# Keys and values from rounded parts of the context, scan units in other slots, a pair's end two slots later, sums over two units

## Time and profile before

| | |
|---|---|
| time, median of 3 runs | 2230.54 us (2229.82 to 2233.25) |
| profiled execution | 2231.84 us, its span 2230.1 us |
| busy in the span | PE 2087.4 us (94%), DVE 1631.8 (73%), ACT 1519.4 (68%), POOL 597.7 (27%) |
| maxima of strips (L989) | 256, 1827 ns each |
| keys (L597), values (L607), turnings (L632) on PE | 399.0, 406.1, 464.4 us busy |

### The profile page before, as it was taken

The page is one execution under the profiler, slowest core; times in us unless marked ns, Lnnn a source line. Parts: engine busy times, 40 slices in busy tenths (PEclk is TensorE's granted clock), DMA queues, the critical chain, the costliest instruction groups (busy, mean ns, idle before and its releaser), DMA issues. The chain is left out here.

```text
span 2230.1 us, 54255 instructions
## 1 busy us (share of the span) xinstructions
PE 2087.4 (94%) x20746; PEld 1431.6 (64%) x20746; DVE 1631.8 (73%) x3522; ACT 1519.4 (68%) x3140; POOL 597.7 (27%) x604
## 2 busy tenths in 40 slices
PE   7999999999999999999999999999998559989965
PEld 4666666666666666666666666666665448868854
DVE  4447777878787878687878787777778747767746
ACT  2667776767686868676767777777768237757753
POOL 0001030303030312122121213030303127767770
PEclk9999999999999999999999999999999569999988
DMA  6475762213232222222222222221201147666748
GB/s 214 172 264 213 263 215 102 98 48 101 63 92 74 73 74 73 75 76 74 72 79 67 83 75 87 77 93 53 99 16 60 63 132 222 211 223 210 220 131 339
DMA packets 114271, 277.26 MB, mean 124 GB/s; under 512 B 19851, under 2 KB 70711, under 8 KB 107872
## 3 DMA queue, kind: packets, MB, share of 16 engines
q1 hardware_dynamic: 95584, 239.10, 32.7%
q0 software_dynamic: 18432, 34.69, 4.4%
HBM read 165.40 MB, written 108.27 MB: 123 GB/s over the span
## 5 line engine op out<-in xcount | busy, mean ns | idle before, releaser
L989 DVE TENSOR_REDUCE sb_negmax<-S 128x1 f32<-128x1604 f32 x256 | 467.7, 1827 | 145.6 <-PE S L622 139.7
L808 ACT ACTIVATE sb_probsT<-W 128x384 f32<-128x384 f32 (+1 forms) x1024 | 476.1, 516 | 90.7 <-PE W L632 86.5
L816 ACT ACTIVATE sb_probs<-S,sb_negmax 128x1604 f32<-128x1604 f32 x256 | 409.3, 1599 | 113.1 <-DVE sb_negmax L989 113.0
L632 PEld LDWEIGHTS W<-sb_ident,sb_probs 128*128 128x128 f32 (+1 forms) x3328 | 365.4, 139 | 185.8 <-ACT sb_K L800 133.3
L632 PE MATMUL W<-sb_ident,sb_probs 128*128 128x128 f32 (+1 forms) x3328 | 464.4, 278 | 6.5 <-ACT sb_probsT L808 2.5
L607 PE MATMUL W<-sb_wkv_in,sb_ctx 128*128 128x256 f32 (+1 forms) x1664 | 406.1, 386 | 14.3 <-ACT sb_probsT L808 12.4
L597 PE MATMUL W<-sb_ctx,sb_wkv_in 128*32 128x401 f32 x4096 | 399.0, 503 | 1.5 <-DMA sb_ctx<-ctxT 1.5
L800 ACT ACTIVATE sb_K<-W,sb_pair_cols 128x401 f32<-128x401 f32 x256 | 152.7, 596 | 279.9 <-PE W L597 279.8
L607 PEld LDWEIGHTS W<-sb_wkv_in,sb_ctx 128*128 128x128 f32 (+1 forms) x1664 | 293.4, 187 | 74.2 <-ACT sb_probsT L808 38.2
L1369 POOL DMA_INDIRECT y_scratch<-sb_ys,sb_places x256 | 254.0, 992 | 109.1 <-issue 74.4
L622 PE MATMUL S<-sb_K,sb_Q 32*128 32x400 f32 (+1 forms) x2048 | 244.3, 546 | 7.3 <-ACT sb_probs L816 6.1
(11 more groups left out here) (197 smaller groups left out, 2813.4 us busy)
## 6 DMA issues: line engine op xcount, KB each, us to landing
sb_ctx<-ctxT SPq DMA_DIRECT2D x32, 1604.0 KB, 7.6
xe_scratch<-sb_none SPq DMA_DIRECT2D x32, 1088.0 KB, 12.2
sb_xg<-xe_scratch SPq DMA_DIRECT2D x64, 544.0 KB, 4.1
sb_BC<-bc_scratch SPq DMA_DIRECT2D x32, 1024.0 KB, 6.2
sb_Q<-sb_q_own SPq DMA_DIRECT2D x128, 128.0 KB, 4.1
y_scratch<-sb_none SPq DMA_DIRECT2D x16, 1024.0 KB, 12.0
sb_rows<-y_scratch SPq DMA_DIRECT2D x16, 1024.0 KB, 8.1
sb_wgu<-wgu SPq DMA_DIRECT2D x64, 192.0 KB
```

What stands on the lines that cost most here:

```text
L632: ins = pe.transpose(W[0:keys_in(t), at * P:(at + 1) * P], probs[n % 2][:, t * P:t * P + keys_in(t)], ident[:])
L808: act.activation(probsT[k][n % (k + 1)][:, 0:wide], ring[bank_of("T", G, k)][:, 0:wide], ACT.Copy)\
L816: act.activation(probs[n % 2][:].rearrange("p (c k) -> p c k", c=QUADS), scores_of, ACT.Exp, bias=negmax[:, slot:slot + 1], accum_out=den[ ...
L989: dve.tensor_reduce(negmax[:, slot:slot + 1], scores_of, AX.XY, ALU.max, negate=True).then_inc(max_done, 1)
```

## The change

*Rounded parts.* The weights of keys and values and each batch's context are split into a rounded part (float32r, written by a ScalarE copy) and a remainder (VectorE subtraction, also float32r). Keys and values are made of three products, hi x hi, lo x hi and hi x lo, by two feature halves: six matmuls in place of two. The context comes in quarters of 402 columns (128 x 804 elements with both feature halves) into one buffer; `part_ctx` (ScalarE) and `part_low` (VectorE) take a quarter in the slots of `PART_AT`, SyncE loads the next batch's quarter in the slots of `LOAD_AT`.

*Keys of four strips at once.* A job K is now one quarter of the context for all 128 features of a group, so four jobs give four strips. They go to K_f, and SyncE deals each strip's 32 rows with four transfers into one of four K tiles. Keys are made six strips ahead (`LEAD`) in place of four.

*Slots.* The scan units move to `UNIT_AT`; the end of a pair (m 13 to 15) comes two slots later (`LATE`), yT in slot 3, ln3T and logits in slot 4, the choice in slot 5; values move from slots 1 to 7 and 9 to 15 to slots 2 to 8, 10 to 15 and 0; XQ and Q move to slot 9, Q behind the keys.

*Sums.* Two units' products are added first, then summed over states once; three instructions per unit become four per two units.

The diff, its core:

```diff
-NO_VALUES = (0, 8)
+NO_VALUES = ()
-CK = (M + QUADS - 1) // QUADS
+CK = 2 * ((M + 2 * QUADS - 1) // (2 * QUADS))
+LEAD = 6
+OF = 4
+PART_AT = {1: (1, 0), 2: (1, 1), 3: (1, 2), 4: (1, 3), 7: (2, 0), 8: (2, 1), 10: (2, 2), 11: (2, 3)}
+LOAD_AT = {2: (2, 0), 3: (2, 1), 4: (2, 2), 5: (2, 3), 8: (3, 0), 9: (3, 1), 11: (3, 2), 12: (3, 3)}
+LATE = 2
+END = SLOTS * (PAIRS + 1) + LAG + LATE
 MIX = {(4, 0): ["O3"], (5, 0): ["oqT"], (5, 1): ["proj"], (6, 0): ["ln2T"], (6, 1): ["xp"], (7, 0): ["dt"],
-       (8, 0): ["XQ"], (8, 1): ["Q"], (10, 0): ["O0"], (14, 0): ["O1"], (1, 0): ["yT"],
-       (2, 0): ["O2", "ln3T"], (2, 1): ["logits"], (3, 2): ["pos"]}
+       (9, 0): ["XQ"], (9, 2): ["Q"], (10, 0): ["O0"], (14, 0): ["O1"], (2, 0): ["O2"], (3, 0): ["yT"],
+       (4, 1): ["ln3T"], (4, 2): ["logits"], (5, 2): ["pos"]}
-FIRST_DECAY = 4
-SUMMED_LATE = (0, 1, 2)
+UNIT_AT = (5, 6, 8, 9, 11, 12, 13, 14)
+def late_at(G):
+    p, m = mixer_at(G - LATE)
+    return (p, m) if m > 12 else (None, m)
-    if 1 <= slot <= 7 and i < PAIRS:
-        return i, 1, slot - 1
-    if slot >= 9 and i + 1 < PAIRS:
-        return i + 1, 0, slot - 9
+    if 2 <= slot <= 8 and i < PAIRS:
+        return i, 1, slot - 2
+    if slot >= 10 and i + 1 < PAIRS:
+        return i + 1, 0, slot - 10
+    if slot == 0 and 0 < i < PAIRS:
+        return i, 0, len(V_UNITS) - 1
...
-START = [("K", 0), ("K", 1), ("XQ", 0), ("K", 2), ("Q", 0), ("K", 3)]
+START = [("K", 0), ("K", 1), ("XQ", 0), ("K", 2), ("Q", 0), ("K", 3), ("K", 4), ("K", 5)]
...
+            def load_ctx(batch, c):
+                after(sp, ctx_lo_up, (batch - 1) * QUADS + c + 1 if batch > 0 else 0)
+                own = slice(c * CK, (c + 1) * CK)
+                sp.dma_start(ctx_t[:, :, own], io["ctxT"][batch, :, own].rearrange("(k p) m -> p k m", p=P)).then_inc(ctx_in[c], 16)
+            def deal_keys(n):
+                four, s = divmod(n, STRIPS)
+                sp.wait_ge(ring_free["act"], free_at("K", four * QUADS + QUADS - 1))
+                after(sp, s_done, n - OF + 1)
+                for c in range(QUADS):
+                    sp.dma_start(K[n % OF][32 * c:32 * c + 32, :], K_f[four % 2][32 * s:32 * s + 32, c, :]).then_inc(k_in[n % OF], 16)
...
             for G in range(END):
+                if G + 2 < ALL_STRIPS:
+                    deal_keys(G + 2)
...
             for i in range(PAIRS + 2):
-                if ended:
-                    pool.wait_ge(dve_up, dve_at(i - 2, "V3"))
-                    pool.tensor_tensor(st[:, 17:18], st[:, 16:17], neg_half[:], ALU.pow)...
                 if nxt:
                     rstd_q(i + 1)
+                if ended:
+                    pool.wait_ge(late_up, routed_at(i - 2, "V3"))
+                    pool.tensor_tensor(st[:, 17:18], st[:, 16:17], neg_half[:], ALU.pow)...
...
             def k_mm(n):
-                for k in range(DT):
-                    for c in range(QUADS):
-                        ins = pe.matmul(W[32 * c:32 * c + 32, 0:CK], wkv_in[:, k, w0:w0 + 32],
-                                        ctx_t[b][:, k, c * CK:(c + 1) * CK], start=(k == 0), stop=(k == DT - 1))
+                pe.wait_ge(ctx_lo_up, batch * QUADS + c + 1)
+                products = [(w, x, k) for w, x in ((wkv_hi, ctx_hi), (wkv_lo, ctx_hi), (wkv_hi, ctx_lo)) for k in range(DT)]
+                for at, (w, x, k) in enumerate(products):
+                    ins = pe.matmul(W[:, 0:CK], w[:, k, g * P:(g + 1) * P], x[:, k, c * CK:(c + 1) * CK],
+                                    start=(at == 0), stop=(at == len(products) - 1))
             def v_mm(pair, b, unit):
-                    for k in range(DT):
-                        ins = pe.matmul(W[0:keys_in(t), n * D:(n + 1) * D], ctx_t[b][:, k, t * P:t * P + keys_in(t)],
-                                        wkv_in[:, k, D:2 * D], start=(k == 0), stop=(k == DT - 1))
+                    for at, (x, w, k) in enumerate(products):
+                        ins = pe.matmul(W[0:keys_in(t), n * D:(n + 1) * D], x[:, k, t * P:t * P + keys_in(t)],
+                                        w[:, k, D:2 * D], start=(at == 0), stop=(at == len(products) - 1))
             def scores(n):
-                pe.wait_ge(ring_free["act"], free_at("K", n))
+                pe.wait_ge(k_in[n % OF], 16 * QUADS * (n // OF + 1))
...
+            def part_ctx(batch, c):
+                act.wait_ge(ctx_in[c], 16 * (batch + 1))
+                if batch > 0:
+                    act.wait_ge(ring_full, full_at("K", (batch - 1) * 2 * QUADS + QUADS + c))
+                own = slice(c * CK, (c + 1) * CK)
+                act.activation(ctx_hi[:, :, own], ctx_t[:, :, own], ACT.Copy).then_inc(ctx_hi_up, 1)
...
                     turned(G, 0)
                     turned(G, 1)
+                if part_at(G, PART_AT):
+                    part_ctx(*part_at(G, PART_AT))
...
+            def part_low(batch, c):
+                dve.wait_ge(ctx_hi_up, batch * QUADS + c + 1)
+                own = slice(c * CK, (c + 1) * CK)
+                dve.tensor_tensor(ctx_lo[:, :, own], ctx_t[:, :, own], ctx_hi[:, :, own].bitcast(F32), ALU.subtract).then_inc(ctx_lo_up, 1)
...
             def sum_unit(p, unit, link):
-                link(dve.tensor_tensor(mine[:, 0:2, :], mine[:, 0:2, :], mine[:, 2:4, :], ALU.add))
-                link(dve.tensor_tensor(mine[:, 0, :], mine[:, 0, :], mine[:, 1, :], ALU.add))
+                if q % 2 == 0:
+                    return
+                both = bx[:, (q - 1) * QS:q * QS, :]
+                link(dve.tensor_tensor(both, both, bx[:, q * QS:(q + 1) * QS, :], ALU.add))
+                link(dve.tensor_tensor(both[:, 0:2, :], both[:, 0:2, :], both[:, 2:4, :], ALU.add))
+                link(dve.tensor_tensor(both[:, 0, :], both[:, 0, :], both[:, 1, :], ALU.add))
...
                 if slot == 6 and 2 <= i < PAIRS:
                     route_link = route_begin(i - 2)
+                if part_at(G, PART_AT):
+                    part_low(*part_at(G, PART_AT))
-                if slot == 8 and nxt:
+                if slot == 9 and nxt:
                     q_out(i + 1)
```

More of the change, by code:

```diff
@@ L105, in small_at @@
     if i == PAIRS and slot in (3, 4) and place == 0:
-        names = ["O3"] if slot == 3 else []
+        names = ["O3", "yT"] if slot == 3 else []
+    if i == PAIRS and slot == 5 and place > 0:
+        names = ["pos", "proj"] if place == 1 else []
     for name in names:
@@ L157, in held_by, with part_at @@
     return JOBS[NUMBER[job] - BANKS] if NUMBER[job] >= BANKS else None
+def part_at(G, at):
+    i, slot = divmod(G, SLOTS)
+    if slot not in at:
+        return None
+    ahead, c = at[slot]
+    return (2 * i + ahead, c) if 2 * i + ahead < BATCHES else None
 def multiplied_at(n, t):
@@ L245, in mixer_phase @@
         neg_half = sb("neg_half", [P, 1])
[L248 removed]
+        K_f = [sb(f"K_f{n}", [P, QUADS, CK]) for n in range(2)]
+        K = [sb(f"K{n}", [P, CK]) for n in range(OF)]
         V = [sb(f"V{n}", [P, KT, D]) for n in range(2)]
@@ L319, in mixer_phase @@
         w_mm = sem("w_mm")
-        ctx_in = [sem(f"ctx_in{n}") for n in range(2)]
+        ctx_in = [sem(f"ctx_in{n}") for n in range(QUADS)]
+        wkv_hi_up = sem("wkv_hi_up")
+        wkv_lo_up = sem("wkv_lo_up")
+        ctx_hi_up = sem("ctx_hi_up")
+        ctx_lo_up = sem("ctx_lo_up")
+        k_in = [sem(f"k_in{n}") for n in range(OF)]
         x_in = sem("x_in")
@@ L794, in _ @@
             act.preload_act_table_set("natural_log_exp_and_others")
+            def part_ctx(batch, c):
[4 more added lines that the diff above has]
+                act.activation(ctx_hi[:, :, own], ctx_t[:, :, own], ACT.Copy).then_inc(ctx_hi_up, 1)
             def k_up(n):
-                _, g, s = step_of(n)
+                four, c = divmod(n, QUADS)
+                g = four % DT
                 act.wait_ge(ring_full, full_at("K", n))
-                after(act, s_done, n - STRIPS + 1)
-                act.activation(K[:, s, :], ring[bank_of("K", n)][:, 0:CK], ACT.Identity,
-                               bias=pair_cols[:, g * STRIPS + s:g * STRIPS + s + 1]).then_inc(ring_free["act"], 1)
+                if c == 0 and four >= 2:
+                    for half in range(OF):
+                        act.wait_ge(k_in[half], 16 * QUADS * (four - 1))
+                act.activation(K_f[four % 2][:, c, :], ring[bank_of("K", n)][:, 0:CK], ACT.Identity,
+                               bias=k_cols[:, g:g + 1]).then_inc(ring_free["act"], 1)
             def turned(G, k):
@@ L837, in _ @@
             act.wait_ge(kv_in, 16 * len(kv_loads))
-            for n in range(STRIPS):
+            act.activation(wkv_hi[:], wkv_in[:], ACT.Copy).then_inc(wkv_hi_up, 1)
+            for c in range(QUADS):
+                part_ctx(0, c)
+            for n in range(LEAD):
                 k_up(n)
@@ L914, in bank @@
                 return ring[bank_of(*job)]
-            for c in range(1, QUADS):
```

(2 more changed lines are left out.)

205 lines of the change are left out of this document (119 added, 86 removed).

## The result

The changed kernel takes 2307.93 us (median of 4 runs, 2306.86 to 2309.45) against 2231.4 (2229.82 to 2233.25): a ratio of 1.0344, 95% interval 1.0331 to 1.0357. It is 76.5 us slower, where 2234 was forecast. Its profiled execution took 2309.45 us, span 2307.7, 77.6 longer than before's.

A forecast was written before the change was run, and what follows sets the result against it. TensorE was taken to bound the phase, VectorE 20 us per pair behind. A +1.6 and B -1.1 made +0.5 a pair, +6.5 over thirteen; with the ends +2, so 2231.8 became 2234 us, range 2165 to 2290.

The forecast's parts named there:

- A: Steady pair from the maximum of slot 1 to that of slot 12: forecast 78.0 us, 1.6 longer than before.
- The route in slot 8: VectorE in slot 8: the route meets the second half of GpSimd's block, 3.6 us instead of 2.3, +1.3.
- the dearer case: A VectorE remainder starting inside GpSimd's block would, by the lock rule, wait up to 1.2 us.
- the second rival: Dealt keys come late, behind clears and broadcasts in SyncE's queue: 2270 to 2320 us, slower; 15%.
- The four units after the last maximum: At the end, four scan units remain where two did: 11.8 us against 6.2, +5.7.
- what VectorE still waits for in A, 8.1 us: VectorE's idle waits in slots 1 to 11, walked strip by strip, sum to 8.1 us a pair.
- 1.10 us for keys and 0.72 for a tile, taken from the pace of the expert phase: TensorE's rounded matmuls: keys from 1.47 to 1.10 us, a tile of values from 0.865 to 0.72, saving 9.7 a pair.
- Stretch B, 1.1 shorter: Slots 12 to 15 and 0, bound by TensorE: forecast 29.4 us, 1.1 shorter than before.
- ends and tail: First pair -9, second -6, last +2.5, units after the last maximum +5.7, start +2 us.
- The first (the gain gets through): Rival: VectorE's waits hide and TensorE's saving shows in the time, 2090 to 2195 us; 27%.
- The third: Rival: rounded matmuls run no faster than the keys and values they replace; +5 us a pair, 2300 us; 8%.

The follow-up runs named there:

- the old order: Changed kernel with scan units and the end of a pair back in their former slots, rounded parts, dealt keys and sums over two units kept: 2231.95 us, ratio 0.9997.

## Why the prediction was wrong

**Right.** VectorE took A over, and at its forecast work: 66.3 us busy where 67.7 were worked out. Slot 2 has 9.25 us (9.0 worked out) and slot 11 its 4.8 us of chain. The route in slot 8 met GpSimd's second half, with the forecast 1.2 us twice:

```profile
1084.81 1.21 DVE L1278 TENSOR_SCALAR sb_topf<-sb_topf 128x8 f32<-128x8 f32 x1
1086.05 1.20 DVE L1279 TENSOR_TENSOR scores_all<-sb_top,sb_topf 128x8 f32<-128x8 f32 x1
```

GpSimd's block ended at 1087.23, and the remainder of that slot began at 1088.18, free of it; all 128 remainders took 0.99 us on average. So the lock held as in the earlier trace rows and as the Trainium skill (SBUF — State Buffer, Who interferes with whom) has it, but the dearer case, a remainder beside a multiplication of GpSimd, didn't come up here. It does in the old order, where the remainder of slot 11 lasts 2.19 in place of 0.99 in all thirteen steady pairs:

```profile
1064.90 2.19 DVE L1067 TENSOR_TENSOR sb_ctx_lo<-sb_ctx,sb_ctx_hi 128x804 fp32r<-128x804 f32 x1
...
1064.94 1.29 POOL L572 TENSOR_TENSOR sb_bx<-sb_u,sb_BC 128x512 f32<-128x512 f32 x1
```

The dealt keys were on time, against the second rival: one score in the whole run waits for a transfer, 0.3 us, and a deal lands in 2.9 us (KB each, median us to landing):

```profile
sb_K<-sb_K_f SPq DMA_DIRECT2D x1024, 50.2 KB, 2.9
```

The four units after the last maximum stand there as forecast, one after the other, their scans at 1791.86, 1795.77, 1799.76 and 1802.59 behind a maximum at 1789.97.

**The step that failed: what VectorE still waits for in A, 8.1 us.** It measured 11.4 in the pair shown, and the steps between instructions 2.8 where 2.2 were put: 66.3 + 11.4 + 2.8 = 80.5, in place of 78.0; over all pairs the mean is 81.2. The waits were in the right places and most too small: logits 2.27 (1.8), Q and O0 2.0 (1.35), xp 1.43 (1.15), maxima 2.9 (2.1), the exponential behind exp(7) 0.8 (0.6); waits for values and the copy of ln3T, 1.4, weren't in the sum. All but two of them are waits for TensorE. One term beneath is **1.10 us for keys and 0.72 for a tile, taken from the pace of the expert phase; 1.30 and 0.76 here**. I took the best of the rows as the pace and left out that the first rounded matmul of a group takes longer, which happens once or twice a strip here. The run with one product for keys shows that the waits at the logits and ahead of the maximum of slot 4 follow the price of keys almost one to one. It also shows that the waits at xp, Q and O0 don't: xp was 1.43 before, and putting it at 1.15 had no ground.

**Stretch B, 1.1 shorter, was wrong in sign**: 31.2 in place of 29.4. The order costs 2.0 there and the faster matmuls give back 1.2. TensorE fills B, so its price counts in full: with 1.30 and 0.76 the sum of five strips and nine tiles is 5 x 0.20 + 9 x 0.04 = 1.4 higher, 30.8, which is 1.4 of the 1.8 missing. A and B together miss by 3.2 + 1.8 = 5 us a pair, 65 us in all; ends and tail make up the rest (the first pairs give 9.4 where 15 were forecast, the last costs 4.6 for 2.5, the tail 9.9 for 5.7). Of the tail, 8.6 us lie ahead of x3, where the four units wait 1.9 us for ScalarE's decays; the rest lies in the phases behind.

**Unforeseen: the clock.** In stretch A, TensorE's waits of 1.3 and 1.7 us in slots 4 and 5 are sometimes followed by half its clock. The same stretch of slot 5 in two pairs, from the projection on:

```profile
836.96:841.70 4.74, 4.74 (x36) 3.47 (x36) 3.19 (x18) 1.94 (x4) 0.55 (x1) 0.64 0.01 3
1063.20:1066.40 3.20, 3.20 (x36) 2.42 (x36) 2.78 (x17) 1.94 (x4) 0.00 (x0) 1.00 0.00 0
```

The same 36 instructions take 4.74 us at a granted clock of 0.64 (part of them at 1.2 GHz) and 3.20 at 1.00; the strip takes 8.25 in place of 6.99. In both pairs the same two waits, 1.26 and 1.68 us, came before, so what decides stays open. About 20 us of the steady pairs ran at 1.2 GHz, so it explains 10 us at most of the 76 (six pairs, 1.5 us longer each: 9); the steady pairs before and in the old order had none. By pairs without a fall, A is 80.5 us: 2.5 of its miss of 3.2 are waits and work, 0.7 the clock.

**The rivals.** The first (the gain gets through) fell: in the old order, at its best, it is nil. The third, that the matmuls run no faster, gave 2300 us for a mechanism that is only half true: they run faster, by just over half of what I took, and VectorE doesn't idle before most maxima (before three of A's eleven, 2.9 us). That its number came near was luck. The time also lies in the second rival's range, 2270 to 2320, but not by its mechanism. The forecast weighed the whole change against 8 us of waits, with a range of its own of 2 us a pair; the miss was 5 us a pair.

Shown by undoing them: the place of the logits (37 us) and of the units (38 us), 70 us together. Shown by taking them away: the remainders (60 us in the new order, about 9 of it the clock's; 45 in the old). Shown by a shorter group of keys: that their price sets the wait at the logits. Open: what makes the waits at xp, Q and O0 what they are, and when the clock falls.

## What to carry to other kernels

When work moves from the engine that bounds a stretch to another, count the idle time that it has left strip by strip, and also what the two engines exchange within a strip: a result that VectorE needs early must stay ahead of the next batch of matmuls, however cheap these have become. Try the new order and the new arithmetic apart from each other: here the arithmetic was worth nothing in the old order and the order cost 65 us on its own. Sort the repeats of a pattern by whether the clock fell in them before comparing means: one edit here looked worse by 10 us, and its repeats without a fall were shorter. A price taken from another phase is a lower end until a row of this shape, with these neighbours, shows it.

## What the runs showed of the hardware

The first pair of rounded matmuls behind float32 ones took 0.32 us where the next took 0.24 (256 columns), and 0.47 against 0.38 (402 columns). GpSimd's subtraction of 804 elements lasts 1.91 us against VectorE's 0.99, and holds VectorE's scans: 1.23 us became 1.70 on average, and one beside a subtraction of 1.92 took 3.21. VectorE's subtraction beside one multiplication of GpSimd (1.29) took 2.19. TensorE's granted clock fell from 2.4 to 1.2 GHz in a phase in which TensorE is busy 91% of a pair, and in a kernel with less work on TensorE it fell more (0.951 over the span against 0.968). A pair with one fall took 1.5 us longer than one without (113.1 against 111.6).
